# A two-layer decoder on one core: the causal mask laid by ScalarE in the first attention, and reordered stage borders

## What is computed

```python
x = x + L0_attn(ln(x))        # 16 heads of 128, rotary, causal softmax, own inner norm and residual
x = x + L0_retention(ln(x), ctx)
x = x + L0_sparse_ffn(ln(x))  # 64 tiles in 8 clusters, argmax, splines
x = x + L1_window_attn(ln(x)) # 16 heads of 16, a band of 64
x = x + L1_cross_attn(ln(x), ctx)
x = x + L1_moe(ln(x))         # 16 experts, 8 taken
```

```python
q, k, v = (x @ w.T + b for w, b in ...)      # each to 16 x 128 x 16 heads x 128
q, k = rope(q), rope(k)
attn = einsum('bihd,bjhd->bhij', q, k) / sqrt(128)
attn = where(causal, -inf, attn)
o = einsum('bhij,bjhd->bihd', softmax(attn), v)
return o.reshape(b, s, 2048) @ wo.T + bo + residual
```

## Time and profile before

| | |
|---|---|
| Median of 3 runs | 1048.48 us (1046.69 to 1048.58) |
| Profiled execution | 1046.12 us |
| its span, first to last instruction | 1044.3 us |
| mean granted TensorE clock | 0.982 of full speed |
| TensorE busy | 987.1 us |
| VectorE busy | 772.3 us |
| ScalarE busy | 701.9 us |
| GpSimd busy | 330.7 us |

### The profile page before, as it was taken

The page is one execution under the profiler, slowest core; times in us unless marked ns, Lnnn a source line. Parts: engine busy times, 40 slices in busy tenths (PEclk is TensorE's granted clock), DMA queues, the critical chain, the costliest instruction groups (busy, mean ns, idle before and its releaser), DMA issues. The chain is left out here.

```text
span 1044.3 us, 19330 instructions
## 1 busy us (share of the span) xinstructions
PE 987.1 (95%) x6896; PEld 818.3 (78%) x6925; DVE 772.3 (74%) x1525; ACT 701.9 (67%) x1959; POOL 330.7 (32%) x276
## 2 busy tenths in 40 slices
PE   7999999999999999999999988699999989899997
PEld 3898888888998899889988866577777789774444
DVE  5798867667676676776757989899998644567774
ACT  5888876777767776776662358487788535448882
POOL 1343333322333233323310120054545310106672
PEclk9999999999999999999999998999999999899999
DMA  7322000000000001000205000000000000018652
GB/s 211 94 61 61 1 2 1 2 1 1 2 1 1 1 2 36 2 1 1 82 16 132 1 1 1 1 2 2 1 2 2 2 1 2 8 51 277 217 180 81
DMA packets 31841, 40.21 MB, mean 39 GB/s; under 512 B 8193, under 2 KB 23297, under 8 KB 31745
## 3 DMA queue, kind: packets, MB, share of 16 engines
q1 hardware_dynamic: 31744, 38.98, 11.9%
HBM read 36.74 MB, written 2.23 MB: 37 GB/s over the span
## 5 line engine op out<-in xcount | busy, mean ns | idle before, releaser
L349 POOL TENSOR_TENSOR roped_q<-roped_q,sin_q 128x512 f32<-128x512 f32 x64 | 82.0, 1281 | 302.3 <-DVE sin_q L494 302.3
L1664 ACT ACTIVATE win_P<-banks,win_neg_max 128x128 f32<-128x128 f32 x256 | 91.4, 382 | 27.6 <-DVE win_neg_max L1740 27.3
L349 POOL TENSOR_TENSOR roped_k<-roped_k,sin_k 128x512 f32<-128x512 f32 x64 | 83.2, 1301 | 46.6 <-DVE sin_k L494 46.6
L403 ACT ACTIVATE P<-banks,neg_max 128x128 f32<-128x128 f32 x256 | 90.5, 372 | 6.9 <-DVE neg_max L519 6.6
L437 ACT ACTIVATE oT_hi<-banks,bv_col 128x512 fp32r<-128x512 f32 x64 | 44.1, 690 | 74.2 <-PE banks L667 74.2
L1601 POOL TENSOR_TENSOR win_P<-win_P,win_inv 128x512 f32<-128x512 f32 x64 | 66.9, 1046 | 70.4 <-DVE win_inv L1745 70.3
L412 ACT ACTIVATE sin_k<-banks 64x512 f32<-64x512 f32 x128 | 76.0, 594 | 11.6 <-PE banks L37 10.1
L522 DVE SCALAR_TENSOR_TENSOR oT_lo<-banks,bv_col,oT_hi 128x512 fp32r<-128x512 f32 x64 | 47.9, 749 | 42.6 <-ACT oT_hi L437 42.0
L412 ACT ACTIVATE sin_q<-banks 64x512 f32<-64x512 f32 x128 | 76.0, 594 | 2.9 <-PE banks L37 0.7
L629 PE MATMUL banks<-WO_lo,oT_hi 128*128 128x256 f32 x256 | 72.9, 285 | 0.0
L493 DVE SCALAR_TENSOR_TENSOR roped_k<-banks,qk_bias,cos 128x512 f32<-128x512 f32 x64 | 48.0, 750 | 33.2 <-ACT sin_k L412 33.2
(11 more groups left out here) (428 smaller groups left out, 3141.2 us busy)
## 6 DMA issues: line engine op xcount, KB each, us to landing
ret_V<-moe_gate_rows SPq DMA_DIRECT2D x16, 512.0 KB, 4.8
ctx<-moe_gate_rows SPq DMA_DIRECT2D x16, 512.0 KB, 5.2
X<-in_x SPq DMA_DIRECT2D x4, 512.0 KB, 6.6
stage<-in_wqT SPq DMA_DIRECT2D x4, 512.0 KB, 4.1
stage<-in_wvT SPq DMA_DIRECT2D x4, 512.0 KB, 5.9
stage<-in_woT SPq DMA_DIRECT2D x4, 512.0 KB, 4.3
ctx<-in_ctxT SPq DMA_DIRECT2D x4, 512.0 KB, 5.8
out<-X SPq DMA_DIRECT2D x8, 256.0 KB, 2.4
```

What stands on the lines that cost most here:

```text
L349: nc.gpsimd.tensor_tensor(roped[w][:, p, :], roped[w][:, p, :], sin_part[w][:], ALU.add).then_inc(roped_sum[w], 1)
L403: ins = nc.scalar.activation(P[:, i, :], SC[:, i * 128:(i + 1) * 128], ACT.Exp, bias=neg_max[:, r % 2, i:i + 1], accum_out=exp_sum[:, r % ...
L1664: ins = nc.scalar.activation(P[:, h % 2, s, i, :], SC[2 * (h % 2) + s][:, i * 128:(i + 1) * 128], ACT.Exp, bias=neg_max[:, h % 2, at:at + ...
```

## The change

1. Attention: the mask product stays for step 0 alone. From then on ScalarE writes the mask into SC (`lay_mask`, an activation Copy of 128x512 from bf16), after its own exponentials and sin_q of the step; the score products wait for that (semaphore mask_laid).
2. Attention's start: chunk 3 is rounded and split in step 1 (between the halves q and k) and no longer behind step 0, chunk 4 behind step 1, chunks 5 and 6 in step 2 (split in step 3). keep_busy(7) stands for keep_busy(4).
3. Local attention's front: k before q; V goes to the bank OT and waits for nothing; split_k and split_q come ahead of batches 4 to 6; xT of pair 1 is rounded ahead of the ticks and split in tick 0; batches 5 to 15 are finished by a table (FINISHED) and part 1 behind tick 2; the identity times band comes ahead of the waits for q and k in `score`.
4. Borders: 8 matmuls that nobody reads at the end of phase_spline, 5 at the end of phase_window, 4 at the end of phase_cross; split_front comes ahead of the last addition.

The diff, cut to its core:

```diff
@@ phase_attn0
         def rounded_at(r):
-            return [i for i in ((3, 4) if r == 0 else (r + 4,)) if i < len(ITEMS)]
+            return [i for i in ((), (4,), (5, 6))[r:r + 1] or ((r + 4,),) for i in i if i < len(ITEMS)]
         def split_at(r):
-            return [i for i in (r + 3,) if i < len(ITEMS)]
+            return [i for i in ((), (), (4,), (5, 6))[r:r + 1] or ((r + 3,),) for i in i if i < len(ITEMS)]
...
+                def lay_mask(u):
+                    if live(u, STEPS - 1):
+                        act.wait_ge(exps_done, u + 1)
+                        nc.scalar.activation(SC[:].rearrange("p (h n) -> p h n", h=GROUP), four(mask[:]), ACT.Copy).then_inc(mask_laid, 1)
...
                             ins.then_inc(rotated[w], 1)
+                            if w == 0:
+                                lay_mask(u)
...
+                            if s == 1 and w == 0:
+                                round_weights(STAGES + 1)
+                    else:
+                        lay_mask(u)
...
                         rope(s, r % 2, r, 0)
+                        if s == 1:
+                            split_weights(STAGES + 1)
                         rope(s, r % 2, r, 1)
                     if g == 0:
-                        if r == 0:
-                            split_weights(STAGES + 1)
...
-                    wait(pe, exps_done, u)
                     if u == 0:
                         pe.wait_ge(consts_made, 2)
-                    nc.tensor.matmul(SC[:], ident_b[:], four(mask[:]), start=True, stop=True)
+                        nc.tensor.matmul(SC[:], ident_b[:], four(mask[:]), start=True, stop=True)
+                    else:
+                        pe.wait_ge(mask_laid, u)
...
-                keep_busy(4)
+                keep_busy(7)
@@ phase_spline, TensorE's last work
+                pe.wait_ge(win_rounded, 1)
+                for _ in range(8):
+                    nc.tensor.matmul(bank[0], kept["win_qk_hi"][:, 0, 0:128], kept["win_qk_hi"][:, 0, :], start=True, stop=True)
@@ phase_window
+        FINISHED = 5, 6, 7, None, 8, 9, 10, 11, None, 12, None, 13, None, 14, None, 15
+        PART_AT = {2: 1, 8: 2, 16: 3}
...
+                    values = PREP[(i + 1) % 2] if i > 0 else OT
...
+                round_k(0)
                 round_q(0)
-                round_k(0)
                 act.wait_ge(V_cleared, 1)
                 take_v(0)
+                round_xT(1)
...
                 finish_part(0)
+                split_k(0)
+                split_q(0)
+                normalise(1)
                 finish_batch(4)
-                normalise(1)
-                finish_batch(5)
-                split_q(0)
-                finish_batch(6)
-                split_k(0)
...
+                    if h == 0:
+                        split_xT(1)
...
+                    if h < len(FINISHED) and FINISHED[h]:
+                        finish_batch(FINISHED[h])
+                    if h in PART_AT:
+                        finish_part(PART_AT[h])
...
                 def score(h):
+                    wait(pe, exps_done, 2 * (h - 1))
+                    for s in range(2):
+                        nc.tensor.matmul(SC[2 * (h % 2) + s], ident_b[:], flat(band[:]), start=True, stop=True)
                     if h % 4 == 0:
                         pe.wait_ge(q_lo_ready, i + 1)
                         pe.wait_ge(k_lo_ready, 2 * i + 2)
...
+                project_k(0)
                 project_q(0)
-                project_k(0)
                 project_v(0)
...
+                keep_busy(5)
@@ phase_cross
                     add_out(2 * i)
+                    if i == PAIRS - 1:
+                        split_front()
...
-                split_front()
...
+                for _ in range(4):
+                    nc.tensor.matmul(SC[0], qk_hi[:, 0, 0, 0:128], qk_hi[:, 0].rearrange("p k n -> p (k n)"), start=True, stop=True)
```

More of the change, by code:

```diff
@@ L215, in phase_attn0 @@
         exps_done = sem("exps_done")
+        mask_laid = sem("mask_laid")
         inv_ready = sem("inv_ready")
@@ L1592, in power @@
                     return nc.gpsimd.tensor_tensor(rstd[:, some], var_eps[:, some], minus_half[:, some], ALU.pow)
-                for part in range(2):
-                    pool.wait_ge(stat, stat_done[part])
-                    power(PARTS[part]).then_inc(rstd_ready, 1)
+                pool.wait_ge(stat, stat_done[0])
+                power(PARTS[0]).then_inc(rstd_ready, 1)
                 for h in range(TICKS):
@@ L1602, in _ @@
                                                 ALU.mult).then_inc(probs_ready, 1)
-                    if h in (7, 15):
-                        part = 2 + h // 8
+                    if h in (1, 7, 15):
+                        part = 1 + (h + 1) // 8
                         pool.wait_ge(stat, stat_done[part])
@@ L1652, in take_v @@
                     wait(act, weighed, 8 * (i - 1))
+                    values = PREP[(i + 1) % 2] if i > 0 else OT
                     for ql in range(2):
-                        src = PREP[(i + 1) % 2].rearrange("p (h l a d) -> p h l a d", l=2, a=2, d=DH)[:, :, ql]
+                        src = values.rearrange("p (h l a d) -> p h l a d", l=2, a=2, d=DH)[:, :, ql]
                         dst = V[:, i % 2].rearrange("p b (h l a) d -> p (b h) l a d", l=2, a=2)[:, :, ql, :, DH * ql:DH * ql + DH]
@@ L1685, in _ @@
                         take_v(m)
-                    if p > 0 and m + 1 < PAIRS + CROSS:
+                    if p > 0 and m + 1 < PAIRS + CROSS and h != 1:
                         (round_xT, round_q, round_k)[p - 1](m + 1)
@@ L1783, in _ @@
                         take_PT(h - 3, 1)
-                    if p == 1 and m + 1 < PAIRS + CROSS:
+                    if p == 1 and 0 < m < PAIRS + CROSS - 1:
                         split_xT(m + 1)
@@ L1802, in _ @@
                         restat(m - 2)
-                    if p == 2 and m + 2 < PAIRS + CROSS:
+                    if p == (2 if m > 0 else 3) and m + 2 < PAIRS + CROSS:
                         normalise(m + 2)
-                    if h == 0:
-                        finish_batch(7)
-                        finish_part(1)
-                    if h % 2 == 1 and h < 16:
-                        finish_batch(8 + h // 2)
-                    if h in (8, 16):
-                        finish_part(1 + h // 8)
+                    if h < len(FINISHED) and FINISHED[h]:
+                        finish_batch(FINISHED[h])
+                    if h in PART_AT:
+                        finish_part(PART_AT[h])
                     if p == 1 and m == 5:
@@ L1818, in transpose_x @@
                     pe.wait_ge(xn_ready, 2 * i + 2)
-                    wait(pe, V_ready, i)
+                    if i == 1:
+                        pe.wait_ge(q_lo_ready, 1)
+                    else:
+                        wait(pe, V_ready, i)
                     for k in range(KD):
@@ L1852, in project_v @@
                 def project_v(i):
-                    if i < PAIRS:
+                    if 0 < i < PAIRS:
                         pe.wait_ge(q_lo_ready, i + 1)
-                    else:
+                    elif i >= PAIRS:
                         pe.wait_ge(cross_q_ready, i - PAIRS + 1)
@@ L1862, in project_v @@
                                 x, weight = (cr_xT_hi[:, i - PAIRS, k, j], cr_xT_lo[:, i - PAIRS, k, j]), (kept["cr_vo_hi"][:, k, :], kept["cr_vo_lo"][:, k, :])
-                            ins = matmul3(nc, PREP[(i + 1) % 2][:, j * D:(j + 1) * D], x, weight, first=(k == 0), last=(k == KD - 1))
+                            ins = matmul3(nc, (PREP[(i + 1) % 2] if i > 0 else OT)[:, j * D:(j + 1) * D], x, weight, first=(k == 0), last=(k == KD - 1))
                     ins.then_inc(v_projected, 1)
@@ L1880, in score @@
                         pe.wait_ge(k_lo_ready, 2 * i + 2)
-                    wait(pe, exps_done, 2 * (h - 1))
-                    for s in range(2):
-                        nc.tensor.matmul(SC[2 * (h % 2) + s], ident_b[:], flat(band[:]), start=True, stop=True)
                     for k in range(KD):
```

## The result

The changed kernel takes **1039.92 us** (median of 4 runs, 1038.96 to 1041.06) against 1048.53 us (1046.69 to 1048.59) of the kernel before: ratio 0.9923, 95% interval 0.9905 to 0.994.

The account below looks back on a forecast made before the run. TensorE, busy 95% of the span, was taken as the bound, above all in layer 0's attention. The terms 12.0 + 2.4 + 3.0 + 0.8 + 1.5 = 19.7 us, off 1047.5, gave 1027.8 us, range 1020.5 to 1036.5.

Parts of the forecast that it names:

- mask in the attention: Layer 0's attention: moving 63 mask products from TensorE to ScalarE gains 13.5 - 1.5 = 12.0 us; bounds 4.4 and 13.5.
- start: Attention's start: reordered roundings remove TensorE's wait for V and the clock dip, 3.7 us; net 2.4 us, bounds 0.5 and 4.
- local attention: Front of local attention: the new order brings the first maximum 3.0 us sooner; 3.0 us gained, bounds 0.5 and 5.
- window to cross: Border after local attention: five fillers keep TensorE's clock up, gaining 0.8 us (0 to 1.5).
- cross to experts: End of cross-attention: earlier split_front gains 1.0 us and the clock behind it 0.5; 1.5 us in all (0.8 to 2.5).
- The mask's price and the saving per product: Attention step: the mask write costs ScalarE 0.60 us; each mask product removed saves TensorE 0.215 us.
- 63 x 0.215 us = 13.5 us, all on the path: Attention: removing 63 mask products shortens the path by 13.5 us as long as TensorE stays the bound.
- I take 0.5 us in three steps, none in the others, thus 1.5 us given back: Attention's first 16 steps, with weight chunks: ScalarE's mask delays TensorE in three steps only, costing 1.5 us.
- PT's cushion: Quiet attention step: PT needed at 263.3, TensorE ready to weigh at 263.6; the cushion shrinks to 0.3 us but holds.
- rival A: Attention: the ring ScalarE to VectorE becomes the bound, period about 7.95 us, 4.4 us won instead of 12.0; 1035.4; chance 0.13.
- Rival D: Attention: ScalarE's bank write costs far more than a read, program slower from 1.28 us a write; chance 0.04 with anything like it.
- rival C: Borders and front give nothing, as later statistics push VectorE back and fillers run past other engines' end; 1033; chance 0.11.

Follow-up runs that it names:

- e1: The changed kernel with the mask product back on TensorE in all 64 steps, none laid by ScalarE: 1037.86 us, ratio 0.9928.
- e7: On e1, the four edits of the roundings' order at the attention's start undone: 1037.81 us, ratio 0.9907.
- c1: The changed kernel itself, unedited, timed again in another group of runs: 1040.65 us, ratio 0.9936.
- e3: The changed kernel with ScalarE laying the mask only where its queue had room (39 or so scores), TensorE elsewhere: 1034.03 us.
- e2: The kernel before with only ScalarE laying the mask for 63 of 64 steps, nothing else of the change: 1051.54 us, ratio 1.0055.
- e9: On e1, local attention's band products put behind the waits for q and k again: 1040.34 us, ratio 0.9935.
- e12: On e1, split_front put behind the loop of cross-attention again, its four fillers kept: 1040.95 us, ratio 0.994.
- e4: On e1, the 8 + 5 + 4 filler products at the three borders taken out: 1040.33 us.
- e5: The changed kernel with VectorE laying the mask, behind its product of P, instead of ScalarE: 1034.76 us, ratio 0.988.

## Why the prediction was wrong

| term | forecast | measured |
|---|---|---|
| mask in the attention | -12.0 | +2.8 (after against e1; +3.1 on the kernel before) |
| start | -2.4 | -1.45 (e7 against e1, a fall of the clock included) |
| local attention | -3.0 | -3.0 after, -4.4 in c1 and e1 |
| window to cross | -0.8 | -0.6 |
| cross to experts | -1.5 | -3.1 |

The mask's term is wrong by 14.8 us and in sign; without it the forecast would have been 7.7 us off, and the other four together measured 8.1 in the profiles. That they add up so well is in part luck: the start gave less and the end of cross-attention twice as much as forecast.

**The mask's price and the saving per product** were right: 583 ns, and 0.215 us where a single mask goes (e3). The sum over 62 steps is 13.3 us. Of it 62 x 0.055 = 3.4 us never came, since two laid masks in a row gain 0.16 us a step, with ScalarE as with VectorE; the step "63 x 0.215 us = 13.5 us, all on the path" was too high by that.

**The step that failed** is "I take 0.5 us in three steps, none in the others, thus 1.5 us given back". It is 12.7 us in 25 of the 62 steps, 8.2 of it behind the first group: 13.3 - 3.4 - 12.7 = -2.8. I had followed one quiet step's queue and one loaded step, and took a mean over 100 us, ScalarE busy 74, for the state of each. That mean hides that ScalarE waits for the maximum and then owes PT at a fixed time: the idle time that covers the mask is behind the exponentials, and each thing that makes these late (the constant, a chunk, a copy of xT) takes it away first. The earlier trace rows showed it, PT following the k copy with no wait, and I priced it in the first group only. I also let each mask press on one step alone; where steps with much work follow each other, the late k copy makes VectorE's next maximum late too, and the two add up to 1.4 us, as ahead of score 21.

**PT's cushion** was mis-sized too. I set the weighing at 263.6 us against PT at 263.3; with the earlier mask product's removal counted once more it is 263.4, and the cushion 0.1 us, not 0.3. In quiet steps it held (7.88 us with ScalarE's mask and with VectorE's), so rival A, a ring that binds in every step, was not the case either. Rival D's sign was right for this part (e2: slower) by a mechanism that I had not priced: not the write's length (583 ns), but its place in the queue.

**The start**: the first score came 2.8 us sooner, with no wait of TensorE for V. PT in step 2 came late as worked out (1.24 us of wait, 1.4 forecast), but the maximum and PT were late at the scores 5 and 8 too, which the net of 2.4 leaves out. And the fall of the clock, 1.5 us of the term, is not bound to the wait: e2 waited as long and had none.

**Local attention**: the first maximum comes 3.8 us sooner behind the block's start, where I had 3.0, and the first PT 6.4 us sooner. Of that 3.4 are given back by 707 us in e1 (4.8 in the profiled run of the change, where the clock was 0.89 from 680 to 696 us; 3.4 in c1, at 1.00), and another 1.4 are won at the three late pairs. The postponed statistics hold VectorE, as in rival C: it was busy 22.3 of the 24 us from 672 to 696 us, 19.9 before. TensorE's waits from 655 to 710 us in the changed kernel (us in total, times, longest), and those that stood there before:

```profile
PE banks L1933 <- DVE win_PT L1775: 3.3, 4, 1.7
PE banks L1921 <- DVE win_PT L1775: 1.0, 2, 0.5
```
```profile
PE banks L35 <- DVE win_q_lo L1726: 2.5, 1, 2.5
PE banks L35 <- DVE win_xT_lo L1722: 2.3, 1, 2.3
```

The band products ahead of the waits, which I put inside the 3.0 and left unpriced, are worth 1.8 (e9). That the term came out at 3.0 in the profile of the change is luck.

**The end of cross-attention** was mis-sized by half. The split gives the 1.0 us forecast at the block's end and 0.8 more up to the last moe_XT_lo (e12), and the fillers 0.7 (e4); the remaining 0.6 us no run parts.

## What to carry to other kernels

Before work is put on an engine that waits a quarter of its time, find the steps in which it does not: a shift pays only in steps whose own cushion, measured between the late input and the engine's next deadline, is longer than the work. Follow the work's delay into the next step as well, through the other engines. Where the load differs from step to step, choose the engine per step; the same 0.6 us laid where there is room gave 0.16 us each, and laid everywhere cost 2.8. And move the long item that makes a step late (here an addition with no hurry) before anything is moved in behind it.

## What the runs showed of the hardware

**Short products behind each other cost 0.055 us a step more than the mask's removal should leave.** One quiet step with all masks on TensorE (e1), TensorE, then weight loads; and with VectorE's mask (e5):

```profile
261.31 1.05 PE L663 MATMUL banks<-roped_k,roped_q 128*128 128x128 f32 x8
262.20 1.06 PE L688 MATMUL banks<-PT,V 128*128 128x128 f32 x8
263.02 0.48 PE L35 MATMUL banks<-xT_odd,WQ_hi 128*128 128x512 f32 x1
...
261.10 1.08 PEld L663 LDWEIGHTS banks<-roped_k,roped_q 128*128 128x128 f32 x8
```
```profile
261.28 1.06 PE L651 MATMUL banks<-roped_k,roped_q 128*128 128x128 f32 x8
262.17 1.11 PE L676 MATMUL banks<-PT,V 128*128 128x128 f32 x8
263.04 0.48 PE L35 MATMUL banks<-xT_odd,WQ_hi 128*128 128x512 f32 x1
...
261.17 0.97 PEld L651 LDWEIGHTS banks<-roped_k,roped_q 128*128 128x128 f32 x8
262.13 0.97 PEld L676 LDWEIGHTS banks<-PT,V 128*128 128x128 f32 x8
```

From the scores' start to the first q product it is 1.71 us with the mask product ahead and 1.76 without. In e5 each run of eight loads takes 0.97 us, and eight products start within 0.89 (261.28 to 262.17): the loads are the longer. With the mask product ahead the first load starts 0.21 us ahead of its product (261.10, 261.31), without it 0.11. That this lead is the 0.055 us is my reading; no run tested it alone.

**The granted clock differs between executions of the same code**, and the time with it. The kernel before runs from 1043.3 to 1049.8 us over all its runs at mean clocks of 0.974 to 0.987; each kernel with the new front of local attention stays within 4 us. That the front is the reason is not shown: e2, whose front is that of before, stays within 2.6 us. The places seen in the profiles are behind TensorE's wait at 26 us (0.62 over 4 us before, 1.00 in e2 behind the same wait), from 530 to 560 us (0.94 in e3, 1.00 in e1: 1.8 us up to local attention), from 672 to 688 us (0.54 in e2, 0.89 before: 3.1 us), and near 940 us (0.79 in e4 and e12, 1.00 in the others shown: 1.5 us):

```profile
934.00:942.00 8.00, 6.77 (x32) 2.92 (x32) 5.97 (x9) 4.84 (x11) 4.14 (x3) 0.79 1.04 368
934.00:942.00 8.00, 7.06 (x41) 4.88 (x39) 3.24 (x7) 5.94 (x13) 1.29 (x1) 1.00 0.56 223
```

These are the windows of e4 and of the kernel before. What makes the clock fall in one execution and not in another no run shows. A difference of 1 to 3 us between two such profiles can be this alone; only positions of marks in the trace, stage by stage, told the terms apart.
